# The fifth score tile of three of the four slots moves from the three-bank ring into the fourth work bank

## The chip, the core and the metric

The kernel runs on one core of one Trainium2 chip. Its metric is device time in microseconds (us): the kernel before takes 3530.04 us, the median of 3 runs (3528.82 to 3530.36).

## The reference: attention and a mixture of experts over one normalised input

The input is 8 sequences of 1024 tokens with 256 features. The output is the input, plus attention of the normalised input, plus an expert layer of it (router, 64 experts of which each token takes 8, a shared expert). The change touches attention alone, which is, cut down:

```python
q = (y @ Wq.T + bq)   # 16 heads of 64, for 8 sequences of 1024 tokens
k = (y @ Wk.T + bk)
v = (y @ Wv.T + bv)
att = softmax(einsum('bhqd,bhkd->bhqk', q, k) / 8)
out = einsum('bhqk,bhkd->bhqd', att, v)
out = out @ Wo.T + bo
```

## The kernel before, in words

**Stages.** A first stage normalises, routes and makes the values v. The attention stage, which this document is about, follows, and an output stage multiplies by Wo and adds everything up. The attention stage has 64 steps. One step handles one pair of heads of one sequence, and it also carries the expert work of one expert and the projection of q and k for a later pair. The steps are written out by `run_steps`: steps 0 to 2 stand by themselves, steps 3 to 60 are a hardware loop whose body holds two steps (so 58 steps run through it), and steps 61 to 64 stand by themselves again. In the loop a semaphore is compared with a register, so TensorE's sequencer also computes these registers; outside it the values are constants.

**A step on TensorE** has four slots, g = 0 to 3 ("first" to "fourth slot" below). Each slot is, in this order:

- eight score tiles, n = 0 to 7. One tile is 128 keys x 512 queries of one head: two matmuls, `q_full,k_full` (line 831) and `q_rest,k_rest` (line 834), into one PSUM bank. ScalarE then takes the exponential of the tile (line 1095) and writes it to `probs`. The tile n = 4 is the fifth.
- between these tiles, the items of `ITEMS`: after tile n = 2 the projection PJ (six matmuls, line 936), after n = 3 of the first and third slot a transpose MT (line 908), after n = 4 of the second slot the expert's first product GU (line 921), after n = 5 of the first and fourth slot a transpose XT (line 913) and the expert's last product DN (lines 927 and 928).
- a "quad", number 2g: four matmuls of 512 columns (line 860) into the four work banks. VectorE reduces them to maxima (line 1132), two reduces of 1024 columns for each quad.
- the product of probabilities and values (`pv`, line 875, 16 matmuls), in the first slot behind the sum product (`add_up`, line 886).
- the quad 2g + 1.

**The PSUM banks.** There are eight. Banks 0 to 2 are the ring, used in turn by the score tiles and, once a step, by the sum product. Bank 3 collects the output. Banks 4 to 7 are `work`: the quads take all four; in between PJ uses the first of them, GU, XT and DN the second, MT the third. The fourth, bank 7, is used by the quads alone.

**What sets the order.** Each engine's program is written out by hand, and semaphores tie the engines together. `ring_free` makes a score tile wait until the ring bank that it takes has been read: for the tile or the sum product three places back in the ring. So tile n = 7 of the fourth slot waits for the exponential of tile n = 4. `probs_ready` counts exponentials, `quad_reduced` VectorE's reduces, `y_weighted` ScalarE's copy of DN's result (line 1060), `gate_ready` its three copies of GU's result (lines 1052 to 1054), `lows_ready` VectorE's line 1142 behind each PJ. The waits of the first quad of each slot are in `quad`, and which of them there are depends on the slot. GpSimd adds the exponentials up (lines 1321 and 1322), all through the step, and computes `hidden_e` (line 1310), which DN reads.

Of the kernel before, what the change touches and what calls it, by code (L numbers as in the profile page):

```python
# [22 lines left out]
ACT = mybir.ActivationFunctionType  # L23
# [8 lines left out]
NP = B * PAIRS  # L32
# [570 lines left out]
SLOTS = 4  # L603
# [42 lines left out]
def at_most(v, most):  # L646

    return min(v, most) if isinstance(v, int) else v


def ring_place(g, j):

    return j + (g >= 1)


SUM_PLACE = 8
SPREAD = 8


def ring_before(s, place, fin):  # L660

    if place < RING:
        last = max(m for m in range(SCORES + 1) if m % RING == place)
        return "score", SCORES * (s - 1) + last
    before = place - RING
    if before == SUM_PLACE:
        if fin:
            return "sum", s
        before -= RING
    return "score", SCORES * s + before - (before > SUM_PLACE) + 1  # L670


def one(ap, i, pattern, out):
# [30 lines left out]
def attention_stage(nc, ctx, io, keep):  # L704
# [8 lines left out]
    ring = [psum[:, b, :] for b in range(RING)]  # L713
    out_ps = psum[:, 3, :]
    work = psum[:, 4:8, :]

# [95 lines left out]
    def _(pe):  # L814
        def ring_free(s, place, fin):
            kind, count = ring_before(s, place, fin)
            if not known(count, 1):
                pe.wait_ge(*((probs_ready, at_most(count, SCORES * NP)) if kind == "score" else (sum_copied, count)))

        def score(s, par, fin, g, i, h):  # L820
            half, kt, j = g // 2, GROUP * (g % 2) + i, 8 * g + 2 * i + h
            place = ring_place(g, j)
            out = ring[place % RING]
            ring_free(s, place, fin)
            if j == 0:
                if known(s, 1):
                    pe.wait_ge(ones_row, 1)
                pe.wait_ge(placed, DMA * SHUFFLES * (s + 1))
            keys = slice(kt * P, (kt + 1) * P)
            cols = slice(half * HALF, (half + 1) * HALF)  # L830
            nc.tensor.matmul(out, k_full[:, par, h, keys], q_full[:, par, h, cols], start=True, stop=False)  # L831
            if g % 2 == 0 and i == 0 and h == 0:
                pe.wait_ge(shift_placed[half], DMA * (s + 1))
            nc.tensor.matmul(out, k_rest[:, par, h, keys], q_rest[:, par, half, h, :],  # L834
                             start=False, stop=True).then_inc(scores_ready, 1)

        def quad(s, par, flags, q):

            g = q // 2
            fin, att, nxt, prj = flags  # L840
            if q == 0:
                pe.wait_ge(highs_ready, 4 * (s + 2))
            if q % 2 == 0:
                if prj:
                    pe.wait_ge(lows_ready, 4 * (s + 2) + g + 1)
                if att and g == 0:
                    pe.wait_ge(xt_copied, s + 1)
                    pe.wait_ge(shift_ready[1], s + 1)
                if att and g == 1:
                    pe.wait_ge(gate_ready, s + 1)  # L850
                if g == 2:
                    pe.wait_ge(shift_ready[0], s + 2)
                if att and g == 3:
                    pe.wait_ge(y_weighted, s + 1)
            if not known(QUADS * (s + 1) + 2 * q, 1):
                pe.wait_ge(quad_reduced, QUADS * (s + 1) + 2 * q)
            for part in range(2):
                for h in range(2):
                    rows = slice(DK * h, DK * (h + 1))
                    last = nc.tensor.matmul(work[:, 2 * h + part, :], high[rows, 1 - par, 0, q * P:(q + 1) * P],  # L860
                                            high[rows, 1 - par, 1, part * HALF:(part + 1) * HALF], start=True, stop=True)
                    if part == 1:
                        last.then_inc(quad_filled, 1)
# [171 lines left out]
    @block.scalar  # L1035
    def _(act):
        def item(s, par, g, name):
            if name == "PJ":
                which, half = g % 2, g // 2
                if g == 0 and not known(s, 0):  # L1040
                    act.wait_ge(placed, DMA * SHUFFLES * (s + 1))
                act.wait_ge(pj_filled, 4 * (s + 2) + g + 1)
                nc.scalar.activation(high[:, par, which, half * HALF:(half + 1) * HALF], work[:, 0, :],  # L1043
                                     ACT.Identity, bias=bias[:, par, which:which + 1]).then_inc(highs_ready, 1)
            elif name == "XT":
                act.wait_ge(xt_filled, s + 1)
                nc.scalar.copy(x_et[:].rearrange("p k c -> p (k c)"), work[:, 1, 0:D]).then_inc(xt_copied, 1)
            elif name == "GU":
                act.wait_ge(gu_filled, s + 1)
                if not known(s, 1):  # L1050
                    act.wait_ge(hidden_ready, s)
                nc.scalar.activation(silu[:], work[:, 1, P:3 * P], ACT.Exp, scale=-1.0)
                nc.scalar.copy(up_gate[:], work[:, 1, 0:3 * P])
                nc.scalar.copy(up_rest[:], work[F2:P, 1, 2 * P:3 * P]).then_inc(gate_ready, 1)
            elif name == "DN":
                act.wait_ge(dn_filled, s + 1)
                if not known(s, 2):
                    act.wait_ge(scattered, DMA * (s - 1))

                nc.scalar.activation(y_e[:, par, :], work[:, 1, 0:D], ACT.Copy, scale=x_e[:, par, bass.ds(s + D, 1)]  # L1060
                                     ).then_inc(y_weighted, 1)

        def head():
            act.wait_ge(has_ones, 1)
            for n, part in enumerate(halves):
                mine = slice(n * E // 2, (n + 1) * E // 2)
                nc.scalar.copy(running[part, :], psum[halves[0], 2, mine]).then_inc(running_ready, 1)
                nc.scalar.copy(has[part, 1, :], psum[halves[1], 2, mine]).then_inc(running_ready, 1)

            def first_high(s, g, bank):  # L1070
                which, half = g % 2, g // 2
                act.wait_ge(pj_filled, 4 * (s + 2) + g + 1)
                nc.scalar.activation(high[:, s % 2, which, half * HALF:(half + 1) * HALF], bank,
                                     ACT.Identity, bias=bias[:, s % 2, which:which + 1]).then_inc(highs_ready, 1)

            for g in range(SLOTS):
                first_high(-2, g, psum[:, g, :])
            for n in range(8):
                act.wait_ge(row_filled, n + 1)
                nc.scalar.copy(rows[:, 4 * n:4 * n + 4, :], psum[:, 1 + n % 3, :].rearrange("p (g q) -> p g q", q=P)  # L1080
                               ).then_inc(rows_out, 1)
            for g in range(SLOTS):
                first_high(-1, g, psum[:, SECOND[g], :])
            act.wait_ge(rows_stored, DMA * 4)

        def exp(s, g, i, h):
            kt, j = GROUP * (g % 2) + i, 8 * g + 2 * i + h
            act.wait_ge(scores_ready, SCORES * s + j + 1)
            if h == 0:
                if i == 0 and not known(4 * s + g - 1, 1):  # L1090
                    act.wait_ge(pv_done, 4 * s + g - 1)
                added = 14 * s + max(kt, 1) - (0 if g >= 2 else 7)
                if not known(added, 1):
                    act.wait_ge(sums_added, added)
            nc.scalar.activation(probs[:, kt, h, :], ring[ring_place(g, j) % RING], ACT.Exp, scale=SCALE  # L1095
                                 ).then_inc(probs_ready, 1)

        def empty(p):

            act.wait_ge(sum_filled, p + 1)  # L1100
            if not known(p, 1):
                act.wait_ge(spread, DMA * SPREAD * p)
            nc.scalar.copy(recip[:], ring[SUM_PLACE % RING]).then_inc(sum_copied, 1)  # L1103

        def step(s, par, flags):
            fin, att, nxt, prj = flags
            for g in range(SLOTS):
                for n in range(2 * GROUP):
                    if att:
                        exp(s, g, n // 2, n % 2)  # L1110
                    if ITEMS[g].get(n, "MT") != "MT" and present(ITEMS[g][n], g, flags):
                        item(s, par, g, ITEMS[g][n])
                if g == 0 and fin:
                    empty(s - 1)

        head()
        run_steps(act, step)
# [660 lines left out]
```

## Time and profile before

| what | value |
| --- | --- |
| median of the runs | 3530.04 us (3528.82 to 3530.36) |
| the profiled execution, its own time | 3532.16 us |
| its span in the trace | 3530.4 us |
| TensorE matmul busy | 3450.2 us, 98% |
| TensorE weight load busy | 2076.7 us, 59% |
| VectorE busy | 2426.9 us, 69% |
| ScalarE busy | 1643.5 us, 47% |
| GpSimd busy | 2731.7 us, 77% |
| DMA, mean | 190 GB/s |

The span is what lies between the first and the last instruction of the program, the execution's own time has 1.8 us around it. A matmul's end is modelled, and matmuls overlap, so a busy TensorE is not one without waits: what one matmul really costs is the distance from its start to the start of the next. PEld is the loading of a matmul's weights, which runs ahead of the matmul itself. A lower-case q behind an engine (PEldq) marks its sequencer: such an instruction only waits or computes a register.

### The profile page before, as it was taken

Reading aid. Unit: us, or ns where it says so; the run is one execution under the profiler, and the core shown is the slowest. Engines: PE = TensorE matmul, PEld = TensorE weight load, DVE = VectorE, ACT = ScalarE, POOL = GpSimd, SP = SyncE. Lnnn points to the kernel's source line nnn. Section 1 sums busy time; section 2 is a strip of 40 time slices with the busy share of each in tenths; the row PEclk is TensorE's granted clock in tenths of the full one; section 3 lists DMA queues with packets and bytes.
Section 4 is the critical chain, followed back from the end, with each engine's and each line's share of the span. In section 5 each row is a group of like instructions: output and inputs, shape, how many; then the busy total and the mean of one; then the engine's idle time right before and its main releaser. Section 6 shows DMA issues by size and latency. Waiting matters only on the chain. (4 is left out here: it accounts for less than half of the span.)

```text
span 3530.4 us, 60337 instructions
## 1 busy us (share of the span) xinstructions
PE 3450.2 (98%) x16416; PEld 2076.7 (59%) x16416; DVE 2426.9 (69%) x3127; ACT 1643.5 (47%) x3058; POOL 2731.7 (77%) x2339
## 2 busy tenths in 40 slices
PE   7999799999999999999999999999999999999699
PEld 6888555555555555555555555555555555555487
DVE  7888577667667776776767676666667677666344
ACT  4555344444444444444444444444444444444343
POOL 2111289999999999999999999999999998999421
PEclk9999799999999999999999999999999999999899
DMA  7777856766666666666777677766766666663486
GB/s 246 240 220 218 218 126 161 184 186 184 184 183 184 185 184 184 184 182 182 187 188 188 185 188 188 185 185 180 186 184 186 186 186 184 184 183 95 158 317 226
DMA packets 418253, 669.15 MB, mean 190 GB/s; under 512 B 56288, under 2 KB 222880, under 8 KB 418208
## 3 DMA queue, kind: packets, MB, share of 16 engines
q1 hardware_dynamic: 395424, 637.13, 64.8%
q0 software_dynamic: 14336, 23.08, 3.4%
q10 hardware_dynamic: 8448, 8.39, 0.7%
q8 instruction: 23, 0.38, 0.0%
q14 instruction: 22, 0.18, 0.0%
HBM read 306.91 MB, written 126.12 MB: 123 GB/s over the span
## 5 line engine op out<-in xcount | busy, mean ns | idle before, releaser
L1132 DVE TENSOR_REDUCE merged<-psum 128x1 f32<-128x1024 f32 x1024 | 1205.5, 1219 | 670.3 <-PE psum L860 592.8
L1095 ACT ACTIVATE probs<-psum 128x512 f32<-128x512 f32 x2048 | 1085.0, 600 | 1215.3 <-PE psum L834 1209.3
L1321 POOL TENSOR_TENSOR sums<-sums,probs 128x512 f32<-128x512 f32 x768 | 1001.1, 1303 | 62.4 <-ACT probs L1095 3.3
L1322 POOL TENSOR_TENSOR sums<-sums,probs 128x512 f32<-128x512 f32 x768 | 981.9, 1279 | 0.0
L875 PE MATMUL psum<-probs,v_sb 128*64 128x512 f32 x4096 | 936.1, 599 | 0.0
L831 PE MATMUL psum<-q_full,k_full 128*128 128x512 f32 x2048 | 878.6, 429 | 0.9 <-DVE low L1142 0.9
L834 PE MATMUL psum<-q_rest,k_rest 65*128 65x512 f32 x2048 | 812.6, 397 | 1.4 <-DMA q_rest<-minus_max 1.4
L875 PEld LDWEIGHTS psum<-probs,v_sb 128*64 128x64 f32 x4096 | 271.6, 136 | 563.0 <-issue 501.3
L831 PEld LDWEIGHTS psum<-q_full,k_full 128*128 128x128 f32 x2048 | 388.4, 190 | 197.4 <-issue 75.0
L834 PEld LDWEIGHTS psum<-q_rest,k_rest 65*128 65x128 f32 x2048 | 390.0, 190 | 62.5 <-DMA q_rest<-minus_max 1.7
L936 PE MATMUL psum<-x_t,w_qk 128*128 128x512 f32 x1536 | 409.7, 403 | 12.9 <-DVE merged L1132 6.7
L860 PE MATMUL psum<-high 64*128 64x512 f32 x2016 | 369.9, 444 | 4.2 <-DVE merged L1132 2.4
L936 PEld LDWEIGHTS psum<-x_t,w_qk 128*128 128x128 f32 x1536 | 277.3, 191 | 108.4 <-issue 26.4
L860 PEld LDWEIGHTS psum<-high 64*128 64x128 f32 x2016 | 151.1, 185 | 305.0 <-issue 298.9
L1321 POOL TENSOR_TENSOR sums<-probs 128x512 f32<-128x512 f32 x128 | 164.9, 1288 | 123.2 <-ACT probs L1095 121.5
L1043 ACT ACTIVATE high<-psum,bias 128x512 fp32r<-128x512 f32 x248 | 170.8, 689 | 172.1 <-PE psum L936 144.0
L1142 DVE SCALAR_TENSOR_TENSOR low<-psum,bias,high 128x512 fp32r<-128x512 f32 x256 | 183.0, 715 | 90.9 <-ACT high L1043 88.1
L1163 DVE RECIPROCAL recip<-recip 128x128 f32<-128x128 f32 x256 | 224.3, 918 | 22.7 <-ACT recip L1103 22.7
L1660 PE MATMUL psum<-ot_sb,wo 128*128 128x512 f32 x768 | 187.1, 403 | 21.3 <-ACT ot_sb L1580 21.3
L1660 PEld LDWEIGHTS psum<-ot_sb,wo 128*128 128x128 f32 x768 | 146.1, 192 | 56.7 <-issue 22.2
L1555 POOL TENSOR_TENSOR rest<-x_out,moe_sb 128x1024 f32<-128x1024 f32 x16 | 41.5, 2593 | 174.9 <-DVE y L1617 140.3
L1322 POOL TENSOR_TENSOR sums<-probs 128x512 f32<-128x512 f32 x128 | 163.1, 1274 | 0.0
(154 smaller groups left out, 3079.9 us busy)
## 6 DMA issues: line engine op xcount, KB each, us to landing
x_t<-xt SPq DMA_DIRECT2D x118, 1024.0 KB, 6.8
k_full<-high SPq DMA_DIRECT2D x256, 256.0 KB
v<-values SPq DMA_DIRECT2D x64, 512.0 KB, 3.5
w_qk<-wqk_parts SPq DMA_DIRECT2D x64, 512.0 KB
v_sb<-v SPq DMA_DIRECT2D x64, 512.0 KB, 4.8
q_full<-high SPq DMA_DIRECT2D x128, 256.0 KB
q_full<-low SPq DMA_DIRECT2D x128, 256.0 KB
k_rest<-low SPq DMA_DIRECT2D x128, 256.0 KB
```

The lines of the kernel that those rows point to most:

```text
L831: nc.tensor.matmul(out, k_full[:, par, h, keys], q_full[:, par, h, cols], start=True, stop=False)
L834: nc.tensor.matmul(out, k_rest[:, par, h, keys], q_rest[:, par, half, h, :], start=False, stop=True).then_inc(scores_ready, 1)
L860: last = nc.tensor.matmul(work[:, 2 * h + part, :], high[rows, 1 - par, 0, q * P:(q + 1) * P], high[rows, 1 - par, 1, part * HALF:(part + ...
L875: last = nc.tensor.matmul(out_ps[rows, :], v_sb[:, par, kt, rows], probs[:, kt, h, :], start=(kt == 0), stop=(kt == KT - 1))
L936: last = nc.tensor.matmul(out, w_qk[:, par, which, wp, kd, :], x_t[:, xp, kd, cols], start=(j == 0 and kd == 0), stop=(j == 2 and kd == KD ...
L1095: nc.scalar.activation(probs[:, kt, h, :], ring[ring_place(g, j) % RING], ACT.Exp, scale=SCALE).then_inc(probs_ready, 1)
L1132: nc.vector.tensor_reduce(out=merged[:, col:col + 1], in_=work[:, 2 * h:2 * h + 2, :].rearrange("p b c -> p (b c)"), axis=AX, op=ALU.max, ...
L1142: nc.vector.scalar_tensor_tensor(out=low[:, par, which, cols], in0=bank, scalar=bias[:, par, which:which + 1], in1=f32(high[:, par, which, ...
L1163: nc.vector.reciprocal(recip[:, cols], recip[:, cols]).then_inc(recip_ready, 1)
L1321: nc.gpsimd.tensor_tensor(total[:, 0, :], first[:, 0, :], probs[:, kt, 0, :], ALU.add)
L1322: nc.gpsimd.tensor_tensor(total[:, 1, :], first[:, 1, :], probs[:, kt, 1, :], ALU.add).then_inc(sums_added, 1)
L1660: last = nc.tensor.matmul(psum[:, 2 * par + c, :], wo[:, t, h, c * P:(c + 1) * P], ot[:, par, o, h, :], start=(n == 0), stop=(n == 3 * PAI ...
```

## The change

Three score tiles of a step leave the ring: n = 4 of the second, third and fourth slot (tiles 12, 20 and 28 of 32) are written to bank 7 and read from there. They wait for the reduces of the quad before (`quad_reduced`) in place of a ring bank. The first quad of these slots, which overwrites bank 7, waits in addition for the exponential of that tile (`probs_ready`). The other 29 tiles and the sum product, 30 users in all, take the three ring banks in turn, and each waits for the user three places back in this shorter list.

```diff
+WORK_TILES = tuple(8 * g + 4 for g in range(1, SLOTS))
+RING_TILES = [m for m in range(SCORES) if m not in WORK_TILES]
+USERS = RING_TILES[:SUM_PLACE] + ["sum"] + RING_TILES[SUM_PLACE:]
+assert len(USERS) % RING == 0
 def ring_before(s, place, fin):
-    if place < RING:
-        last = max(m for m in range(SCORES + 1) if m % RING == place)
-        return "score", SCORES * (s - 1) + last
-    before = place - RING
-    if before == SUM_PLACE:
+    user = USERS[place - RING]
+    if user == "sum":
         if fin:
             return "sum", s
-        before -= RING
-    return "score", SCORES * s + before - (before > SUM_PLACE) + 1
+        user = USERS[place - 2 * RING]
+    return "score", SCORES * (s if place >= RING else s - 1) + user + 1
...
+    def score_bank(j):
+        return work[:, 3, :] if j in WORK_TILES else ring[USERS.index(j) % RING]
...
         def score(s, par, fin, g, i, h):
-            place = ring_place(g, j)
-            out = ring[place % RING]
-            ring_free(s, place, fin)
+            out = score_bank(j)
+            if j in WORK_TILES:
+                pe.wait_ge(quad_reduced, at_most(QUADS * (s + 1) + 4 * g, QUADS * NP))
+            else:
+                ring_free(s, USERS.index(j), fin)
...
         def quad(s, par, flags, q):
             if q % 2 == 0:
                 if prj:
                     pe.wait_ge(lows_ready, 4 * (s + 2) + g + 1)
+                if att and 8 * g + 4 in WORK_TILES:
+                    pe.wait_ge(probs_ready, SCORES * s + 8 * g + 5)
...
-            nc.scalar.activation(probs[:, kt, h, :], ring[ring_place(g, j) % RING], ACT.Exp, scale=SCALE
+            nc.scalar.activation(probs[:, kt, h, :], score_bank(j), ACT.Exp, scale=SCALE
```

No instruction is added to or taken from the matmuls, the exponentials or the reduces, and their order stays. What moves are waits, and the register computations that stand with them. Two places follow, both on TensorE in the loop. The first is the fourth slot from DN to the quad, in the kernel before; `REGISTER_ALU` computes a register, and a bracket names the semaphores that an instruction waits for, its own and those of pure waits just ahead of it.

```order
L927 MATMUL psum<-w_d0,hidden_e 128x256 [waits hidden_e_ready,quad_reduced]
L928 MATMUL psum<-w_d1,hidden_e 128x256
L818 REGISTER_ALU
L831 MATMUL psum<-q_full,k_full 128x512 [waits probs_ready]
L834 MATMUL psum<-q_rest,k_rest 128x512
L818 REGISTER_ALU
L831 MATMUL psum<-q_full,k_full 128x512 [waits probs_ready]
L834 MATMUL psum<-q_rest,k_rest 128x512
L845 REGISTER_ALU
L856 REGISTER_ALU [waits y_weighted,lows_ready]
L860 MATMUL psum<-high 128x512 [waits quad_reduced]
```

The same place in the changed kernel, where the lines have moved by 3 to 5:

```order
L932 MATMUL psum<-w_d0,hidden_e 128x256 [waits hidden_e_ready,quad_reduced]
L933 MATMUL psum<-w_d1,hidden_e 128x256
L819 REGISTER_ALU
L834 MATMUL psum<-q_full,k_full 128x512 [waits probs_ready]
L837 MATMUL psum<-q_rest,k_rest 128x512
L819 REGISTER_ALU
L834 MATMUL psum<-q_full,k_full 128x512 [waits probs_ready]
L837 MATMUL psum<-q_rest,k_rest 128x512
L848 REGISTER_ALU
L850 REGISTER_ALU [waits lows_ready]
L865 MATMUL psum<-high 128x512 [waits quad_reduced,y_weighted,probs_ready]
```

The wait for `y_weighted` stood ahead of the second register computation; it now stands behind it, directly ahead of the matmul. The second place is the third slot, from MT to the quad, before:

```order
L908 MATMUL psum<-ident,merged 128x128 [waits quad_reduced]
L818 REGISTER_ALU
L831 MATMUL psum<-q_full,k_full 128x512 [waits probs_ready]
L834 MATMUL psum<-q_rest,k_rest 128x512
...
L845 REGISTER_ALU
L860 MATMUL psum<-high 128x512 [waits quad_reduced,shift_ready0,lows_ready]
```

And now:

```order
L913 MATMUL psum<-ident,merged 128x128 [waits quad_reduced]
L834 MATMUL psum<-q_full,k_full 128x512 [waits quad_reduced]
L837 MATMUL psum<-q_rest,k_rest 128x512
...
L848 REGISTER_ALU
L850 REGISTER_ALU [waits lows_ready]
L865 MATMUL psum<-high 128x512 [waits quad_reduced,shift_ready0,probs_ready]
```

The fifth tile waits for the same count as MT ahead of it and needs no register of its own; the quad has one register computation and one wait more.

## Rows read from the trace of the kernel before

**Rows 1.** The page, part 1: busy time and share of TensorE's matmuls.
```profile
PE 3450.2 (98%) x16416; PEld 2076.7 (59%) x16416; DVE 2426.9 (69%) x3127; ACT 1643.5 (47%) x3058; POOL 2731.7 (77%) x2339
```

**Rows 2.** Stretches (loop; step 62): length, then busy us of PE, PEld, DVE, ACT, POOL.
```profile
557.78:3163.74 2605.96, 2605.72 (x12298) 1456.12 (x12297) 1822.12 (x2088) 1241.84 (x2436) 2372.70 (x2031) 1.00 0.70 185
...
3208.45:3252.33 43.88, 39.93 (x191) 20.11 (x189) 30.60 (x32) 18.86 (x38) 41.11 (x36) 1.00 0.47 116
```

**Rows 3.** Timeline, step 29, third slot, tile n = 5 to quad: start, duration, instruction.
```profile
1753.59 0.39 PE L834 MATMUL psum<-q_rest,k_rest 65*128 65x512 f32 x1
...
1753.74 0.19 PEld L831 LDWEIGHTS psum<-q_full,k_full 128*128 128x128 f32 x1 [0.20 <-ACT probs L1095]
1753.82 0.43 PE L831 MATMUL psum<-q_full,k_full 128*128 128x512 f32 x1
...
1754.28 0.19 PEld L831 LDWEIGHTS psum<-q_full,k_full 128*128 128x128 f32 x1 [0.24 <-ACT probs L1095]
...
1754.62 0.39 PE L834 MATMUL psum<-q_rest,k_rest 65*128 65x512 f32 x1
1754.93 0.50 PE L860 MATMUL psum<-high 64*128 64x512 f32 x2
```

**Rows 4.** Timeline, step 29, second slot, the same stretch of TensorE's program.
```profile
1743.26 0.39 PE L834 MATMUL psum<-q_rest,k_rest 65*128 65x512 f32 x1
...
1744.19 0.40 PE L834 MATMUL psum<-q_rest,k_rest 65*128 65x512 f32 x1
...
1744.52 0.73 PE L860 MATMUL psum<-high 64*128 64x512 f32 x4
```

**Rows 5.** Timeline, step 30, third slot, the same stretch.
```profile
1798.54 0.40 PE L834 MATMUL psum<-q_rest,k_rest 65*128 65x512 f32 x1
...
1799.90 0.50 PE L860 MATMUL psum<-high 64*128 64x512 f32 x2
```

**Rows 6.** Timeline, step 29, third slot: one exponential, of tile n = 4.
```profile
1753.63 0.60 ACT L1095 ACTIVATE probs<-psum 128x512 f32<-128x512 f32 x1
```

**Rows 7.** Waits within the loop: who, for whom, us in total, times, longest.
```profile
POOL sums L1321 <- ACT probs L1095: 112.8, 58, 2.1
...
PEld psum L831 <- ACT probs L1095: 19.5, 82, 0.3
```

**Rows 8.** Timeline, step 29, fourth slot: two exponentials, y_e, last tile, quad.
```profile
1764.01 1.08 ACT L1095 ACTIVATE probs<-psum 128x512 f32<-128x512 f32 x2
...
1765.40 0.47 ACT L1060 ACTIVATE y_e<-psum,x_e 128x256 f32<-128x256 f32 x1 [0.30 <-PE psum L928]
...
1765.71 0.40 PE L834 MATMUL psum<-q_rest,k_rest 65*128 65x512 f32 x1
...
1766.10 0.30 PEld L860 LDWEIGHTS psum<-high 64*128 64x128 f32 x4 [0.43 <-issue]
```

**Rows 9.** The wait for y_weighted by source line: whole trace, then step 29 alone.
```profile
L854 PEldq EVENT_SEMAPHORE  x58: 51/51/51, 597.5 to 3158.6; - x58
...
L854 PEldq EVENT_SEMAPHORE  x1: 51/51/51, 1765.9 to 1765.9; - x1
```

**Rows 10.** Timeline, step 29: second slot's reduces, its fifth tile's weights, third slot's low part.
```profile
1737.98 2.35 DVE L1132 TENSOR_REDUCE merged<-psum 128x1 f32<-128x1024 f32 x2 [1.22 <-PE psum L860]
...
1741.00 0.19 PEld L831 LDWEIGHTS psum<-q_full,k_full 128*128 128x128 f32 x1
...
1753.74 0.72 DVE L1142 SCALAR_TENSOR_TENSOR low<-psum,bias,high 128x512 fp32r<-128x512 f32 x1
```

**Rows 11.** Timeline, first slot, before and after PJ: step 1, then step 29.
```profile
469.54 0.40 PE L834 MATMUL psum<-q_rest,k_rest 65*128 65x512 f32 x1
...
471.18 0.39 PE L831 MATMUL psum<-q_full,k_full 128*128 128x512 f32 x1
...
1727.41 0.39 PE L834 MATMUL psum<-q_rest,k_rest 65*128 65x512 f32 x1
...
1729.19 0.39 PE L831 MATMUL psum<-q_full,k_full 128*128 128x512 f32 x1
```

More of the change, by code:

```diff
@@ L648, in at_most @@
     return min(v, most) if isinstance(v, int) else v
-def ring_place(g, j):
-    return j + (g >= 1)
 SUM_PLACE = 8
 SPREAD = 8
+WORK_TILES = tuple(8 * g + 4 for g in range(1, SLOTS))
+RING_TILES = [m for m in range(SCORES) if m not in WORK_TILES]
+USERS = RING_TILES[:SUM_PLACE] + ["sum"] + RING_TILES[SUM_PLACE:]
+assert len(USERS) % RING == 0
 def ring_before(s, place, fin):
-    if place < RING:
-        last = max(m for m in range(SCORES + 1) if m % RING == place)
-        return "score", SCORES * (s - 1) + last
-    before = place - RING
-    if before == SUM_PLACE:
+    user = USERS[place - RING]
+    if user == "sum":
         if fin:
             return "sum", s
-        before -= RING
-    return "score", SCORES * s + before - (before > SUM_PLACE) + 1
+        user = USERS[place - 2 * RING]
+    return "score", SCORES * (s if place >= RING else s - 1) + user + 1
 def one(ap, i, pattern, out):
```

## The prediction, made before the changed kernel was run

> **What bounds the kernel now.** Read the page's first part first: TensorE shows 98% busy [rows 1], and the view of busy time by stretch says the same of the loop, 2605.72 of 2605.96 us [rows 2]. Taken at its word that leaves a relaxed wait nothing to give. It isn't so, because a matmul's end is modelled and matmuls overlap: a matmul that starts late still touches the one before it. So the timeline is to be read by the distance from start to start. In a third slot the stretch from the last matmul of tile n = 5 to the quad, which is tiles 6 and 7, takes 1754.93 - 1753.59 = 1.34 us [rows 3]. The same matmuls in the second slot of the same step take 1744.52 - 1743.26 = 1.26 us [rows 4], and in the next step's third slot 1799.90 - 1798.54 = 1.36 us [rows 5]. In a fourth slot the last tile's second matmul stands 1766.10 - 1765.71 = 0.39 us ahead of the quad's weights [rows 8], in the second slot 1744.52 - 1744.19 = 0.33 us ahead of the quad [rows 4]. These excesses, a tenth of a us each, are all that TensorE loses around the change. A loop step takes 2605.96 / 58 = 44.93 us [rows 2], so each 0.1 us per step is 5.8 us, or 0.16% of the time.
>
> **What the ring costs, and what the change gives back: third slot.** The weight loads of tiles 6 and 7 sat idle 0.20 and 0.24 us until an exponential ended [rows 3]; in the loop there are 82 such waits, 19.5 us of idle loader [rows 7]. The exponential of tile 4 ends at 1753.63 + 0.60 = 1754.23 [rows 6], and tile 7's weights load at 1754.28 [rows 3]: that is the bank three places back. ScalarE is late there because it puts PJ's result into `high` between the exponentials of tiles 2 and 3. After the change tile 6 waits for the exponential of tile 2 and tile 7 for that of tile 3, one exponential sooner each (two take 1.08 us one behind the other [rows 8]), so both waits go. The loader runs ahead of the matmuls, so most of its idle time is covered; what shows is the excess over the second slot, 1.34 - 1.26 = 0.08 and 1.36 - 1.26 = 0.10 us [rows 3 to 5]. I take 0.09 us, by 58 steps 5.2 us. A difference of differences of starts given to 0.01 us may be off by 0.02, so the bounds are 0.06 us (3.5 us in all) and 0.12 us (7.0 us).
>
> Is something late next in that slot? The quad also waits for `lows_ready`: VectorE's low part ends at 1753.74 + 0.72 = 1754.46 [rows 10], and a quad earlier by 0.09 would start at 1754.84. The exponential of tile 4, the new wait of the quad, ends at 1754.23. Both are over by then. The other two slots of the change have their excess elsewhere or none; the first slot doesn't change.
>
> The Trainium skill, "TensorE: Matmul & The Clock Gate", § Step-by-step: what each phase is for, says that TensorE's queue pulls a weight load ahead of matmuls in flight so that it is hidden. Taken to its end, by that rule a load that is 0.2 us late costs nothing and this term is zero. The trace agrees in part: 0.44 us of idle loader [rows 3] became 0.08 us of lateness. The rest is the term above, and the rule's own result is among the rivals below.
>
> **What moves by accident: fourth slot.** ScalarE's copy y_e ends at 1765.40 + 0.47 = 1765.87, and the quad's weights load at 1766.10 [rows 8]: 0.23 us later, where a load directly behind its wait came 0.05 us after the exponential [rows 3, 6]. The order shows what stands between: the wait for `y_weighted`, then a register computation for the next wait, then the matmul. The pure wait (line 854) shows at 1765.9 in this step, and there is one in each of the 58 loop steps [rows 9]. In the changed kernel the register computations stand ahead of that wait and may run while y_e is still being copied. One sequencer step of the chain goes, so the weights can load well ahead of 1765.71 + 0.33 = 1766.04, the start that the second slot's distance allows. Gain 1766.10 - 1766.04 = 0.06 to 0.07 us (the quad's matmul shows a hundredth behind its weights); 0.07 by 58 is 4.1 us. What is late next is that distance itself, the change from tiles of 128 rows to quads of 64, which every slot shows. Bounds: zero, if it isn't the register but the semaphore that takes the 0.23, and 4.1, since nothing can come earlier than the distance.
>
> **What is added.** (a) Three waits of a tile for `quad_reduced`. In the second slot the reduces end at 1737.98 + 2.35 = 1740.33, the fifth tile's weights load at 1741.00 [rows 10]: 0.67 us to spare. In the third slot MT, which stands ahead, waits for the same count already, and in the fourth the tile comes as late in its slot as in the second. Zero. (b) The quads' wait for the tile's exponential: in the fourth slot two exponentials end at 1764.01 + 1.08 = 1765.09 [rows 8], of tiles 4 and 5, 1.0 us ahead of the quad; in the second slot there is GU's whole evacuation between. Zero. (c) One more register computation ahead of the third slot's quad, and a longer chain of waits there and in the second slot. The trace has no such chain at a quad, so two rows bound it: below, nothing, since the second slot's quad already has two register computations and waits and keeps 0.33 us [rows 4]; above, PJ in the first slot, where the loop has a register computation and two register waits in a row: 1729.19 - 1727.41 = 1.78 us against 471.18 - 469.54 = 1.64 us in step 1, where there are no registers [rows 11], so 0.14 us. I take zero, the nearer row: the chain is as long as the one in the second slot today. If the cover failed in both slots it would be 2 x 0.14 x 58 = 16 us.
>
> **Cover and consumers.** Earlier tiles only help if nobody else sets the pace. GpSimd is busy 2372.70 of 2605.96 us in the loop, and it waits once a step for an exponential of the third slot, 112.8 us in 58 times, 1.9 us each [rows 2, 7]. So it has 1.9 us a step to give and needs 0.16. In step 62 TensorE is busy 39.93 of 43.88 us [rows 2]; it waits there for VectorE and GpSimd, so the deeper ring gives nothing in steps 62 and 63, but GpSimd's chain there starts from the exponential of step 61, and what the loop gained reaches the end.
>
> **The sum.** 5.2 + 4.1 = 9.3 us in the loop, and 0.1 us for the third slots of steps 1, 2 and 61: 9.4 us. Against the profiled execution's own 3532.16 us that is 3522.8; that execution was 2.1 us above the median, so against 3530.04 us it is 3520.6 us, 0.27% less.
>
> **The rivals.**
> 1. Only one of the two gains comes. If the register isn't what delays the fourth slot's quad, 5.3 us remain: 3524.7 us. For it: the 0.23 us are seen at one place alone. Against: a direct wait took 0.05. If instead the ring's waits are hidden or something takes their place, 4.1 remain: 3525.9 us. For it: the loader's lead, as above. Against: 1.34 and 1.36 against 1.26 us. Chance 0.22 and 0.08.
> 2. The change does nothing, since another wait of the quad stands right behind in both slots (`lows_ready` in the third, the copy y_e in the fourth): 3530.0 us. Against it are the 0.38 us of margin above. Chance 0.03.
> 3. Slower: the sequencer becomes the bound ahead of the quads of the second and third slot, each of which has a longer chain of register waits. At the price of PJ's place, 0.14 us each, 16.2 - 9.4 = +6.8 us: 3536.8 us. It outweighs the gain from 9.4 / 116 = 0.08 us a quad. Against it: today's second slot. Chance 0.05.
> 4. More is gained: the third slot's tile 5 and MT also close up, since a register computation goes there, which would take away the 0.02 us by which step 30 is longer than step 29 [rows 3, 5], 1.2 us: 3519.4 us. Chance 0.07, beside the forecast.
>
> **How the numbers follow.** The forecast has 0.55, with 3518 to 3523 us as its own range. The 8 in 10 take in rival 4 and most of rival 1: 3517.5 to 3526.0 us. No change is what lies within 0.2%, 7.1 us, of before: 3523.0 to 3537.1 us. Below that are the forecast but for a part of its lower half, and rival 4: 0.53 + 0.07, and a sixth of rival 1, together 0.64. Rivals 1, 2 and most of 3 are no change: 0.33. Slower: 0.03.
>
> **What would show it.** Right: in the timeline of a third slot the stretch from tile 5 to the quad at 1.26 to 1.28 us with no loader idle on an exponential; the waits of line 834's weight loads for exponentials gone from the loop; in the fourth slot 0.33 us from the last tile to the quad; a step of 44.77 us. Wrong: second slot's quad at more than 0.33 us (rival 3), a fourth slot still at 0.39 to 0.40 us (rival 1), a tile waiting for `merged`, or a third slot whose quad now waits for `low`.

## The result, and the profile of the changed kernel

The changed kernel takes 3519.54 us, the median of nine runs (3518.58 to 3522.26); the kernel before, run beside it, 3529.52 us (3528.47 to 3532.01). The ratio is 0.9971, with a 95% interval of 0.9963 to 0.998. So the gain is 7 to 13 us, 10.0 by the medians. The forecast was 3520.6 us. The profiled execution of the changed kernel took 3522.26 us, 9.90 us less than before's profiled 3532.16.

Page, part 1, of the changed kernel, to be read against [rows 1]:

```profile
PE 3440.7 (98%) x16416; PEld 2087.4 (59%) x16416; DVE 2442.0 (69%) x3127; ACT 1644.5 (47%) x3058; POOL 2732.9 (78%) x2339
```

Nothing here says what changed: 98% of a shorter span is still 98%. The view by stretch says where the time went. Its columns are those of [rows 2], ending with the granted clock, the DMA share and GB/s; first the loop, steps 3 to 60, then step 62:

```profile
557.14:3153.96 2596.82, 2596.82 (x12298) 1466.61 (x12297) 1838.12 (x2088) 1242.30 (x2436) 2373.07 (x2031) 1.00 0.70 185
3198.68:3244.18 45.50, 41.98 (x190) 21.41 (x189) 29.37 (x32) 19.19 (x38) 42.61 (x37) 0.96 0.45 112
```

The loop lost 2605.96 - 2596.82 = 9.14 us of the 9.90; another 0.64 us is the head, which ended at 557.14 instead of 557.78 (in the executions profiled below it ends anywhere from 555.2 to 558.5 us, so that is no effect of an edit). A step went from 44.93 to 2596.82 / 58 = 44.77 us.

The third slot of step 29, the stretch of [rows 3], of the changed kernel. First TensorE's matmuls from tile 5's last to the quad, then the weight loads:

```profile
1748.59 0.40 PE L837 MATMUL psum<-q_rest,k_rest 65*128 65x512 f32 x1
1748.83 0.40 PE L834 MATMUL psum<-q_full,k_full 128*128 128x512 f32 x1
...
1749.53 0.39 PE L837 MATMUL psum<-q_rest,k_rest 65*128 65x512 f32 x1
1749.85 0.73 PE L865 MATMUL psum<-high 64*128 64x512 f32 x4
```

```profile
1748.59 0.19 PEld L834 LDWEIGHTS psum<-q_full,k_full 128*128 128x128 f32 x1
...
1749.06 0.19 PEld L834 LDWEIGHTS psum<-q_full,k_full 128*128 128x128 f32 x1
1749.30 0.19 PEld L837 LDWEIGHTS psum<-q_rest,k_rest 65*128 65x128 f32 x1
1749.85 0.30 PEld L865 LDWEIGHTS psum<-high 64*128 64x128 f32 x4 [0.36 <-ACT probs L1100]
```

From tile 5 to the quad it is now 1749.85 - 1748.59 = 1.26 us, against 1.34 [rows 3], and the loads of line 834 show no idle ahead of them. One thing misleads: the quad's weights are shown as idle 0.36 us until an exponential ended. The view of waits over the loop has this as a new entry, and the entry of [rows 7] for tiles is gone:

```profile
POOL sums L1326 <- ACT probs L1100: 103.6, 58, 1.9
...
PEld psum L865 <- ACT probs L1100: 20.7, 58, 0.4
```

It isn't a new bound. The exponential that this quad now needs is that of tile 4, which ended at 1748.63 + 0.60 = 1749.23 us, 0.62 us ahead of the weights:

```profile
1748.63 0.60 ACT L1100 ACTIVATE probs<-psum 128x512 f32<-128x512 f32 x1
...
1749.13 0.59 ACT L1100 ACTIVATE probs<-psum 128x512 f32<-128x512 f32 x1
```

The one that ended last before the load, at 1749.72 (second row), is tile 5's, on which the quad doesn't wait. The distance decides: 1749.85 - 1749.53 = 0.32 us from the last tile is the least that any slot's first quad shows in the loop.

The fourth slot of step 29, for [rows 8]:

```profile
1760.30 0.47 ACT L1065 ACTIVATE y_e<-psum,x_e 128x256 f32<-128x256 f32 x1 [0.30 <-PE psum L933]
...
1760.61 0.40 PE L837 MATMUL psum<-q_rest,k_rest 65*128 65x512 f32 x1
...
1760.93 0.30 PEld L865 LDWEIGHTS psum<-high 64*128 64x128 f32 x4 [0.37 <-issue]
```

From the end of y_e to the weights it is 1760.93 - 1760.77 = 0.16 us instead of 0.23, and from the last tile 0.32 instead of 0.39. Averages over the 58 loop steps, from the starts of the matmuls in the trace (this table has the kernels of the experiments too, each from its one profiled execution; slots that no edit touches differ among them by up to 0.02 us, third slots with the same banks by 0.04):

| us, mean of 58 steps | slot 1 | slot 2 | slot 3 | slot 4 | step | last tile to quad, slot 4 |
|---|---|---|---|---|---|---|
| before | 11.726 | 11.572 | 10.461 | 11.171 | 44.930 | 0.403 |
| changed | 11.724 | 11.577 | 10.376 | 11.096 | 44.773 | 0.329 |
| e1_order_only | 11.723 | 11.574 | 10.454 | 11.101 | 44.852 | 0.329 |
| e2_bank_only | 11.717 | 11.569 | 10.375 | 11.275 | 44.936 | 0.507 |
| e5_bank_one_reg | 11.720 | 11.558 | 10.364 | 11.156 | 44.798 | 0.399 |
| e7_one_wait_behind | 11.721 | 11.571 | 10.387 | 11.179 | 44.859 | 0.413 |
| e4_more_behind | 11.727 | 11.578 | 10.355 | 11.247 | 44.906 | 0.471 |
| e3_pj_order | 11.577 | 11.567 | 10.347 | 11.106 | 44.597 | 0.329 |
| e6_orders_no_bank | 11.566 | 11.566 | 10.478 | 11.091 | 44.701 | 0.329 |

The place of the change in the third slot is steadier than the slot around it. From tile 5's last matmul to the quad, again as the mean of the 58 steps, it is 1.353 to 1.359 us in the three kernels with all tiles in the ring (before, e1, e6) and 1.259 to 1.263 us in the six with the new banks: 0.09 to 0.10 us a step.

### The profile page after: what moved, and what is told of

Its sections match the earlier page's. It is cut to its first block and busy times, and to the rows that moved or that the text cites. A ratio compares the mean times of both kernels' runs of the same rounds, so it can differ in the third digit from the quotient of the medians.

```text
span 3520.5 us, 60349 instructions
## 1 busy us (share of the span) xinstructions
PE 3440.7 (98%) x16416; PEld 2087.4 (59%) x16416; DVE 2442.0 (69%) x3127; ACT 1644.5 (47%) x3058; POOL 2732.9 (78%) x2339
```

## The experiments

Each is compared with the kernel before, in runs on the same chip (its median was 3530.72 us beside e1 to e4, 3529.80 beside e5 to e7). The question: are there two gains, one from the banks and one from the order of waits that came along with them, and is a register computation behind the wait that ends last really what TensorE pays for?

### The order of waits alone (e1_order_only)

```diff
# kernel before, quad(), q % 2 == 0
-                if att and g == 3:
-                    pe.wait_ge(y_weighted, s + 1)
             if not known(QUADS * (s + 1) + 2 * q, 1):
                 pe.wait_ge(quad_reduced, QUADS * (s + 1) + 2 * q)
+            if q == 6 and att:
+                pe.wait_ge(y_weighted, s + 1)
```

> The kernel before, with its ring untouched; in the fourth slot's even quad alone the wait on y_weighted is placed behind the one on quad_reduced, so that both register computations stand ahead of the wait that ends last, as they do after the change. My theory: one register computation less behind the binding wait, the distance from the last score tile to the quad falls from 0.40 to 0.33 us in each of 58 loop steps, 58 x 0.07 = 4.1 us: 3525.4 us against 3529.5 for before; the third slot stays as before (10.41 and 10.50 us). Rival A (the distance is the switch of tile shapes and the semaphore's own delay, not a computation on the sequencer): 3529.5 us, 0.40 us stays. Rival B (the whole gain of the change is this order and the ring is worth nothing): 3519.5 us.

Measured: 3525.89 us, ratio 0.9985 (0.9976 to 0.9994). In the fourth slot the distance to the quad fell to 0.329 us, the third slot stayed at 10.454. Timeline of step 29, fourth slot, e1_order_only:

```profile
1762.15 0.47 ACT L1060 ACTIVATE y_e<-psum,x_e 128x256 f32<-128x256 f32 x1 [0.30 <-PE psum L928]
...
1762.46 0.40 PE L834 MATMUL psum<-q_rest,k_rest 65*128 65x512 f32 x1
...
1762.79 0.30 PEld L860 LDWEIGHTS psum<-high 64*128 64x128 f32 x4 [0.37 <-issue]
```

The weights come 1762.79 - 1762.62 = 0.17 us behind y_e, as in the changed kernel, without any change of banks. The order alone is one of the two gains: 58 x 0.070 = 4.1 us in the fourth slot. Rival A (no gain) and rival B (all of the gain) both lie outside the interval, and fall.

### The banks alone, and what stood behind the wait (e2_bank_only, e5_bank_one_reg)

```diff
# changed kernel, e2_bank_only
-                if att and 8 * g + 4 in WORK_TILES:
+                if att and 8 * g + 4 in WORK_TILES and g < 3:
                     pe.wait_ge(probs_ready, SCORES * s + 8 * g + 5)
...
                 if att and g == 3:
                     pe.wait_ge(y_weighted, s + 1)
+                    pe.wait_ge(probs_ready, SCORES * s + 8 * g + 5)
```

> The changed kernel with its banks and added waits, but in the fourth slot's quad the wait on y_weighted stands ahead of a register computation again, as in the kernel before (and one wait instruction more stands behind it, on quad_reduced, which is long satisfied). My theory: the third slot keeps its gain, 10.41/10.50 to 10.31/10.38 us, 58 x 0.09 to 0.10 = 5.2 to 5.8 us, and the fourth slot's distance from last tile to quad is 0.40 us again, or up to 0.45 if the extra wait instruction costs 0.05: 3524.0 us without, 3527.2 us with it. Rival A (the ring wait was hidden, the gain is all the order's): 3529.5 us. Rival B (the order is worth nothing, the banks all): 3519.5 us.

Measured: 3531.36 us, ratio 1.0001 (0.9992 to 1.001): no gain at all, where I had expected 3524.0 to 3527.2. The slots say why. The third slot has the full gain of the banks (10.375 us), and the fourth gave it all back (11.275 against 11.171). Timeline of step 29, e2_bank_only:

```profile
1765.02 0.47 ACT L1066 ACTIVATE y_e<-psum,x_e 128x256 f32<-128x256 f32 x1 [0.30 <-PE psum L934]
...
1765.33 0.40 PE L837 MATMUL psum<-q_rest,k_rest 65*128 65x512 f32 x1
...
1765.80 0.33 PEld L866 LDWEIGHTS psum<-high 64*128 64x128 f32 x4 [0.52 <-issue]
```

0.31 us from y_e to the weights. The view of one source line shows TensorE's sequencer at work in between, one behind the other, in step 29 (line 859 waits for `y_weighted`, 860 computes a register for `probs_ready`, 862 waits for `quad_reduced`, which was met long before; the duration is in ns, then the start):

```profile
L859 PEldq EVENT_SEMAPHORE  x1: 51/51/51, 1765.5 to 1765.5; - x1
...
L860 PEldq ALU_OP  x1: 32/32/32, 1765.6 to 1765.6; - x1
...
L862 PEldq EVENT_SEMAPHORE  x1: 51/51/51, 1765.7 to 1765.7; - x1
```

My edit had one instruction too many behind the binding wait, and I had put it at 0 to 0.05 us; it cost 11.275 - 11.171 = 0.10. So this run alone couldn't tell "the banks give nothing" from "the banks' gain is paid out again". e5 takes the second wait away by placing `quad_reduced` ahead of `y_weighted`, and leaves exactly one register computation behind, as in the kernel before:

```diff
# changed kernel, e5_bank_one_reg; the probs_ready wait of g == 3 as in e2
                 if att and g == 3:
+                    pe.wait_ge(quad_reduced, QUADS * (s + 1) + 2 * q)
                     pe.wait_ge(y_weighted, s + 1)
-            if not known(QUADS * (s + 1) + 2 * q, 1):
+                    pe.wait_ge(probs_ready, SCORES * s + 8 * g + 5)
+            if not known(QUADS * (s + 1) + 2 * q, 1) and not (att and q == 6):
                 pe.wait_ge(quad_reduced, QUADS * (s + 1) + 2 * q)
```

> The changed kernel with its banks and added waits; in the fourth slot's even quad the waits are ordered so that behind y_weighted stands exactly one register computation, as in the kernel before, without the second wait instruction that the earlier run with the banks alone had there. My theory: third slot 10.38 us (0.085 gained), fourth slot 11.17 us as before, step 44.845 us: 58 x 0.085 = 4.9 us, 3525.8 us against before's 3530.7. Rival (the banks are worth nothing at the end of the program, which is what the earlier run's 3531.4 could also mean): 3530.7 us. Rival (banks worth all): 3520 us.

Measured: 3524.32 us, ratio 0.9985 (0.9976 to 0.9994). Fourth slot 11.156 us, distance 0.399 (0.403 before the change), third slot 10.364. The banks are the other gain, and it reaches the end of the program. In ratios the two parts, 0.9985 each, make 0.9970, and the change has 0.9971. (The profiled execution of e5 was the shortest of its eleven, 3521.97 us; the slots' means are better evidence there than its span.)

### One or two instructions more behind the wait (e7_one_wait_behind, e4_more_behind)

```diff
# changed kernel; e7_one_wait_behind
                 if att and g == 3:
+                    pe.wait_ge(ones_row, 1)
                     pe.wait_ge(y_weighted, s + 1)
# changed kernel; e4_more_behind
                 if att and g == 3:
                     pe.wait_ge(y_weighted, s + 1)
+                    pe.wait_ge(scores_ready, SCORES * s + 9)
+                    pe.wait_ge(highs_ready, 4 * s + 5)
```

In e7 the compiled program puts `y_weighted` into a wait instruction of its own and a second one, on `ones_row` and `quad_reduced`, behind it. All added waits were met long before.

> The changed kernel with one more wait, long met, on a constant (ones_row), in the fourth slot's even quad: behind the instruction that waits for y_weighted stands one more wait instruction, without a register computation. My theory (the sequencer takes about 0.09 us for every instruction behind the binding wait, whatever it is: 39.865 to 39.958 with a register computation, 39.914 and 39.990 with both): fourth slot 11.096 to 11.17 us, 58 x 0.075 = 4.4 us, 3523.9 us. Rival (only the register computation costs, a wait already met is free): 3519.5 us. Rival (a wait instruction costs the 0.10 us that it added in the run with the banks alone, 11.171 to 11.275): 58 x 0.10 = 5.8 us, 3525.3 us.

> The changed kernel with two more waits in the fourth slot's quad, both met long before (on scores_ready and highs_ready, with values held in registers): behind the wait on y_weighted there now stand a fused register computation and one more wait instruction, where in the changed kernel the weight load follows at once. My theory: each instruction that TensorE's sequencer works through behind the binding wait delays the weight load by 0.05 to 0.1 us; distance from last tile to quad 0.33 to 0.43 - 0.50 us, 58 x 0.10 to 0.17 = 6 to 10 us: 3525.5 to 3529.5 us. Rival (such instructions run ahead or beside and cost nothing): 3519.5 us.

Measured: e7 3526.18 us, ratio 0.9989 (0.998 to 0.9998); e4 3528.95 us, ratio 0.9997 (0.9988 to 1.0006). e4 lies in the range of my theory. For e7 the free wait falls (3519.5 us is outside the interval), but the total doesn't decide between the other two prices: 3526.18 us is nearer to the 3525.3 us of a wait at 0.10 us than to my 3523.9, and the interval holds both. The fourth slot grew by 11.179 - 11.096 = 0.083 us, between the two prices and nearer to my 0.075. Timeline of step 29, fourth slot, first e7_one_wait_behind, then e4_more_behind:

```profile
1762.79 0.47 ACT L1066 ACTIVATE y_e<-psum,x_e 128x256 f32<-128x256 f32 x1 [0.30 <-PE psum L934]
...
1763.10 0.40 PE L837 MATMUL psum<-q_rest,k_rest 65*128 65x512 f32 x1
...
1763.48 0.33 PEld L866 LDWEIGHTS psum<-high 64*128 64x128 f32 x4 [0.42 <-issue]
```

```profile
1764.03 0.47 ACT L1067 ACTIVATE y_e<-psum,x_e 128x256 f32<-128x256 f32 x1 [0.30 <-PE psum L935]
...
1764.34 0.40 PE L837 MATMUL psum<-q_rest,k_rest 65*128 65x512 f32 x1
...
1764.78 0.33 PEld L867 LDWEIGHTS psum<-high 64*128 64x128 f32 x4 [0.47 <-issue]
```

From the end of y_e to the weights: nothing behind the wait 0.16 to 0.17 us (changed, e1), where the distance of 0.33 us from the last tile is the bound and hides the rest; one register computation 0.23 (before, [rows 8]); one wait instruction 0.22 (e7); a register computation and a wait instruction 0.28 (e4) and 0.31 (e2). A wait that is already met costs about as much as a register computation: what costs isn't the arithmetic alone, but each instruction of the sequencer between the event and the load. By the table's last column the first costs 0.07 to 0.08 us above the least distance, and the second 0.06 (e4 over e7) to 0.11 (e2 over e5).

### The same cost at another place (e3_pj_order)

If this is so, the first slot has it too: ahead of PJ two register computations stand behind the wait for a reduce.

```diff
# changed kernel, item(), name == "PJ"
-                if nxt and not known(reduced - 1, 1):
-                    pe.wait_ge(quad_reduced, reduced - 1)
                 if which == 0:
                     pe.wait_ge(x_loaded[half], DMA * x_loads(s + 2))
                 if g == 0:
                     pe.wait_ge(w_loaded, 2 * DMA * (s + 3))
+                if nxt and not known(reduced - 1, 1):
+                    pe.wait_ge(quad_reduced, reduced - 1)
```

> The changed kernel, with only the waits ahead of the projection product in each slot reordered: the ones on the loaded x and w first, the one on quad_reduced last. In the first slot of a loop step two register computations (1.368 and 1.463 us into the step) now stand between the reduce that ends the wait (1.329) and the weight load (1.549); in step 1, where these are constants, that load comes 0.053 us behind the reduce. My theory (a register computation behind the binding wait costs about 0.1 us): the product starts 0.15 us earlier in the loop. If nothing takes its place: 58 x 0.15 = 8.7 us, 3510.8 us. If the wait on xt_copied ahead of the next quad takes over, as in steps 1 and 2 (first slot 11.68 us there, 11.73 in the loop): 58 x 0.05 = 2.9 us, 3516.6 us; of these two I take the second. Rival (register computations are free): 3519.5 us.

Measured: 3512.09 us (3509.53 to 3512.46), ratio 0.9943 (0.993 to 0.9957): five runs here, and faster than the changed kernel, by 18.6 against 10.0 us when each is set against the kernel before beside it. Weights of PJ in the first slot of step 29, changed kernel, then e3_pj_order, each behind the last load of the tile ahead:

```profile
1722.11 0.19 PEld L837 LDWEIGHTS psum<-q_rest,k_rest 65*128 65x128 f32 x1
1722.61 0.30 PEld L941 LDWEIGHTS psum<-x_t,w_qk 128*128 128x128 f32 x2 [0.32 <-issue]
```

```profile
1717.74 0.19 PEld L837 LDWEIGHTS psum<-q_rest,k_rest 65*128 65x128 f32 x1
1718.08 0.31 PEld L941 LDWEIGHTS psum<-x_t,w_qk 128*128 128x128 f32 x2 [0.15 <-DVE merged L1137]
```

0.50 us became 0.34. The releaser's name changed as well: "issue" became the reduce itself. The name alone proves little, though: the quads of the changed kernel and of e1 that have nothing behind the wait and stand at the least distance say "issue" too. The first slot fell from 11.724 to 11.577 us, 0.147 by 58 = 8.5 us, close to the larger of my two figures, 8.7 us; I had chosen the smaller, 2.9. The wait on `xt_copied` didn't take over. My reason for it was step 1, where the next quad stands farther from its tile. In e3_pj_order, step 1, then step 29: the copy, the last tile, the quad's weights.

```profile
472.86 0.40 ACT L1052 COPY x_et<-psum 128x256 f32<-128x256 f32 x1
473.01 0.40 PE L837 MATMUL psum<-q_rest,k_rest 65*128 65x512 f32 x1
...
473.43 0.21 PEld L865 LDWEIGHTS psum<-high 64*128 64x128 f32 x2 [0.46 <-issue]
```

```profile
1721.89 0.38 ACT L1052 COPY x_et<-psum 128x256 f32<-128x256 f32 x1
...
1722.38 0.30 PEld L865 LDWEIGHTS psum<-high 64*128 64x128 f32 x4 [0.38 <-issue]
```

Behind the copy's end it is 473.43 - 473.26 = 0.17 us in step 1 and 1722.38 - 1722.27 = 0.11 us in the loop. In step 1 the compiled program has one more wait instruction behind the one on `xt_copied`; in the loop that wait is the last. A step outside a loop isn't a clean stand-in for one inside: here its waits are packed differently.

### Both orders without the banks (e6_orders_no_bank)

The kernel before with the edits of e1 and e3.

> The kernel before with its ring, and both reorderings of waits: y_weighted behind quad_reduced in the fourth slot's quad, and quad_reduced behind the loads' waits in the projection product. My theory (the gains add: 0.07 and 0.15 us a step, and only the banks' 0.08 is missing): step 44.930 - 0.070 - 0.147 = 44.713, 58 x 0.217 = 12.6 us, 3518.1 us against 3530.7 for before. Rival A (the banks' gain is contained in the two others, as a wait that the earlier start shifts away): 3512.1 us, what both orders with the banks gave. Rival B (without the banks the ring wait eats the projection product's gain): 3525.4 us.

Measured: 3519.40 us (3516.84 to 3522.14), ratio 0.9973 (0.9964 to 0.9983). Two reorderings of waits, without the change, do as much as the change did. By the medians that is 10.4 us less than before, where I expected 12.6; the interval, 6.0 to 12.7 us, holds both, and the step of the profiled execution, 44.701 us, is close to the one forecast (44.713). The intervals of the ratios of this run and e3 don't touch, so the banks add to the orders: 18.6 against 10.4 us, each against the kernel before beside it, and by the third slots 58 x (10.478 - 10.347) = 7.6 us. Rival A falls. So does rival B, which had the ring eat the gain in PJ and 3525.4 us: the first slot has it in full, 11.566 us. Loads of the third slot of step 29, e6_orders_no_bank:

```profile
1748.83 0.19 PEld L831 LDWEIGHTS psum<-q_full,k_full 128*128 128x128 f32 x1 [0.27 <-ACT probs L1095]
1748.94 0.19 PEld L834 LDWEIGHTS psum<-q_rest,k_rest 65*128 65x128 f32 x1
1749.49 0.30 PEld L860 LDWEIGHTS psum<-high 64*128 64x128 f32 x4 [0.36 <-issue]
```

The ring's wait is there, 0.27 us of idle loader. The third slots make the banks worth 0.13 us a step here and 0.085 without the new order of PJ. At the place of the change there is no such difference: from tile 5 to the quad it is 1.353 - 1.262 = 0.091 us between e6 and e3, and 1.359 - 1.263 = 0.096 between before and changed. The rest lies elsewhere in the slot and differs among kernels with the same edits too.

## Why the prediction was right

The predicted 3520.6 us was 1.1 us from the median, and the change itself (9.4 us predicted, 10.0 by the medians, 9.14 in the loop) came from the two places named. That the totals meet to 1 us is in part luck, since the interval of the gain is 7 to 13 us wide; the evidence for the mechanism is in the slots.

- **Third slot, 0.09 us a step.** It was 10.461 - 10.376 = 0.085 us, 4.9 us in all. No tile waits for an exponential any more, and the stretch is 1.26 us, both as said; its mean over the loop fell by 0.096 us. e5 shows that it stands by itself.
- **Fourth slot, 0.07 us a step.** It was 11.171 - 11.096 = 0.075 us, 4.4 us. e1 has it alone; e5, e7, e4 and e2 lose it again, with one or two instructions behind the wait. So it is the sequencer and not the semaphore (the first rival falls), and the bound from above, the least distance of 0.33 us, held in all kernels with nothing behind the wait.
- **Added waits, zero.** The second slot stayed at 11.577 us (11.572 before). Its quad stands 0.33 us behind the last tile, and the quad of the third slot 0.32 us. The price named for the slower rival, 0.14 us for PJ's chain, was real: e3 got 0.147 us for it. It didn't strike at the third slot's quad because the chain there was through early: in step 29 its last pure wait started at 1749.5 us, and the weights loaded at 1749.85. Line 861 in the changed kernel, in that quad alone:

```profile
L861 PEldq EVENT_SEMAPHORE  x1: 51/51/51, 1749.5 to 1749.5; - x1
```

- **The rival with more, 3519.4 us.** The median of 3519.54 is nearer to it than to the forecast, but what it named didn't happen. Tile 5 didn't close up: its first matmul starts 0.571 us behind that of tile 4 in the changed kernel's third slots, and 0.569 before (means of the 58 steps), and from tile 3 to tile 4, with MT between them, it is 0.499 us against 0.495. The total alone would have misled.
- **Steps outside the loop.** I expected no gain in step 62. It took 45.50 us instead of 43.88, and I hadn't foreseen that. It isn't the banks: the same banks in e5 took 43.89 us there, and e6, which has none of them, 47.02. Step 62 of e5_bank_one_reg, then of e6_orders_no_bank:

```profile
3198.16:3242.05 43.89, 40.40 (x191) 20.31 (x189) 29.45 (x32) 19.08 (x38) 41.13 (x36) 1.00 0.48 116
```

```profile
3196.01:3243.03 47.02, 43.18 (x191) 21.23 (x189) 30.52 (x32) 18.98 (x38) 44.12 (x38) 0.93 0.45 108
```

  The granted clock accounts for it. Within step 62 of the changed kernel it was 0.50, the lower of TensorE's two levels (1.2 GHz), for 3.40 us; in e6 for 6.80 us. Two stretches of the changed kernel, the one ahead of the fall and the one at the lower level:

```profile
3225.70:3235.70 10.00, 8.29 (x37) 3.78 (x37) 7.37 (x8) 3.15 (x6) 9.63 (x10) 1.00 0.13 44
3235.70:3239.10 3.40, 3.40 (x8) 2.46 (x8) 0.00 (x0) 0.97 (x2) 3.26 (x3) 0.50 0.00 0
```

  The matmuls of that stretch, from the first of DN to the quad, in the changed kernel, then in the kernel before, where the clock stood at 1.00:

```profile
3235.69 1.18 PE L932 MATMUL psum<-w_d,hidden_e 128*128 128x256 f32 x2 [1.18 <-POOL hidden_e L1315]
...
3239.27 0.73 PE L865 MATMUL psum<-high 64*128 64x512 f32 x4
```

```profile
3245.46 0.67 PE L927 MATMUL psum<-w_d,hidden_e 128*128 128x256 f32 x2 [1.86 <-POOL hidden_e L1310]
...
3247.41 0.73 PE L860 MATMUL psum<-high 64*128 64x512 f32 x4
```

  3239.27 - 3235.69 = 3.58 us against 3247.41 - 3245.46 = 1.95 us: 1.63 us, the whole of the 1.62 by which the step is longer.

  TensorE was busy 8.29 of the 10 us ahead of the fall and stood 1.18 us for `hidden_e`. In the kernel before it was no busier at the same place (8.03 of 10.05 us), stood 1.86 us, and kept its clock, so why the clock fell in one and not in the other stays open.

  What the loop gained still reached the end, by the way named: GpSimd's anchor in step 61, its first sum of the third slot that waits for an exponential, came at 3191.32 us before and here at 3181.56, 9.8 us sooner, and its last operation of the program 9.9 us sooner. The 1.62 us of step 62 didn't add to the total: from the start of step 63 to the end it is 3520.50 - 3244.18 = 276.32 us, and 3530.40 - 3252.33 = 278.07 before. Timelines of GpSimd, before, then changed:

```profile
3191.32 1.29 POOL L1321 TENSOR_TENSOR sums<-probs 128x512 f32<-128x512 f32 x1 [1.62 <-ACT probs L1095]
```

```profile
3181.56 1.28 POOL L1326 TENSOR_TENSOR sums<-probs 128x512 f32<-128x512 f32 x1 [1.38 <-ACT probs L1100]
```

  Its idle time there fell by 0.24 us. In the loop its waits for the exponential fell from 112.8 us [rows 7] to 103.6, which is the 0.16 us a step that the prediction said it needs, of the 1.9 us that it had.
- **The weighed rule.** The Trainium skill, "TensorE: Matmul & The Clock Gate", § Step-by-step: what each phase is for, has a weight load pulled ahead and hidden. The runs agree with it in part, as the trace of before did. Taking the ring's 0.44 us of loader idle away gave 0.085 us a step: most of a late load is covered, not all of it.

## What to carry to other kernels

Where an engine waits for several events, put the one that ends last at the end, behind every register computation and behind waits that are met early, and look in the compiled order at what stands between that wait and the instruction: each thing left there cost 0.06 to 0.11 us here, every time round the loop. The sign of it is the time from the end of the event to the load: 0.16 us where nothing stood between and up to 0.31 where two instructions did. A row that says "issue" is a place to look, and no proof. And read an isolating experiment by its slots before its total: e2's total said that the banks are worth nothing, while its third slot said otherwise.

## What was not expected of the hardware

A wait that has long been met isn't free on TensorE's sequencer: behind the binding wait it cost 0.084 us in the distance to the quad (e7, 0.413 against 0.329 us), about what the register computation cost (0.070 in e5, 0.074 in before; that the wait costs more isn't shown, since by the weights it is 0.22 against 0.23 us behind y_e), and the two together cost 0.14 to 0.18 us (e4, e2).
